# Attention stage of a two-layer gated cross-attention kernel: gate folded into the reciprocals, result addition on GpSimd, row statistics and maxima pieces placed anew

## The reference

```python
Q = _split_heads(query, H) * depth ** (-0.5)      # query = _layernorm(x), 2048 rows
K, V = halves of ctx_2048, 1601 rows, split into heads
logits = jnp.einsum('bhqd,bhkd->bhqk', Q, K) + b[0]
logits = logits + -1e+30 * (1.0 - mask)
weights = jax.nn.softmax(logits, axis=-1)
out = jnp.einsum('bhqk,bhkd->bhqd', weights, V)
...
x = x + jnp.tanh(g_xattn[1]) * _L1_xattn_ref(ctx_2048, _layernorm(x, axis=-1), mask_BxS2_ik0, L1_xattn_b)
```

## Time and profile before

| what | before |
|---|---|
| median of three executions | 1227.48 us (1226.67 to 1228.3) |
| the profiled execution, its own time | 1230.68 us |
| its span, first to last instruction | 1228.9 us |
| busy over the span: PE, DVE, ACT, POOL | 1099.3, 785.7, 532.3, 498.0 us |
| mean granted PE clock | 0.947 |
| the attention's first and last score matmul start | 411.0 and 852.0 us |

### The profile page before, as it was taken

The page is one execution under the profiler, slowest core; times in us unless marked ns, Lnnn a source line. Parts: engine busy times, 40 slices in busy tenths (PEclk is TensorE's granted clock), DMA queues, the critical chain, the costliest instruction groups (busy, mean ns, idle before and its releaser), DMA issues.

```text
span 1228.9 us, 20691 instructions
## 1 busy us (share of the span) xinstructions
PE 1099.3 (89%) x7126; PEld 826.5 (67%) x7126; DVE 785.7 (64%) x1804; ACT 532.3 (43%) x1145; POOL 498.0 (41%) x499
## 2 busy tenths in 40 slices
PE   4866999999967799999999999999983999999994
PEld 3665999999964444545455454544753999999994
DVE  5735767666659876767667676854339656565663
ACT  4141444433321345555565655565443333333341
POOL 1641111111104365857566676666002233434342
PEclk9966999999997889999999999999995999999998
DMA  6454787788832000000000000001623566666662
GB/s 225 94 148 182 317 318 289 302 322 336 339 131 86 1 1 1 1 18 1 1 1 18 2 1 2 18 22 50 220 73 112 162 181 211 183 208 198 192 210 57
DMA packets 52754, 160.71 MB, mean 131 GB/s; under 512 B 7434, under 2 KB 38540, under 8 KB 41644
## 3 DMA queue, kind: packets, MB, share of 16 engines
q1 hardware_dynamic: 38590, 138.42, 31.1%
q0 software_dynamic: 12000, 18.36, 6.4%
q10 hardware_dynamic: 2062, 2.60, 0.6%
HBM read 142.97 MB, written 16.38 MB: 130 GB/s over the span
## 4 chain that ended last, share of the span: by engine, by line
PE 78%; DVE 10%; issue 3%; ACT 2%; DMA 1%; POOL 1%; DVEq 0%; ACTq 0%; POOLq 0%
PE PQ L456 25%; PE PB L602 8%; PE PQ L587 7%; PE PB L483 6%; PE PB L569 5%; PE PB L592 4%; DVE Z L1046 4%; PE PB L332 4%; PE PB L502 3%; PE PQ L569 3%; PE PB L482 3%; PE PB L501 2%; PE PQ L643 1%; PE PQ L645 1%; PE PQ L644 1%
## 5 line engine op out<-in xcount | busy, mean ns | idle before, releaser
L1046 DVE TENSOR_REDUCE Z<-PB 128x1 f32<-128x402 f32 x319 | 172.3, 568 | 73.2 <-PE PB L569 71.6
L587 PE MATMUL PQ<-QS,KS 128*128 128x512 f32 x416 | 173.8, 433 | 3.3 <-ACT Z L1315 2.0
L456 PE MATMUL PQ<-Z,WS 128*128 128x128 f32 x1472 | 174.6, 278 | 0.5 <-ACT Z L1227 0.5
L456 PEld LDWEIGHTS PQ<-Z,WS 128*128 128x128 f32 x1472 | 173.1, 194 | 2.2 <-ACT Z L1227 0.9
L1242 ACT ACTIVATE Z<-PQ,W 128x128 f32<-128x128 f32 x312 | 89.0, 368 | 160.0 <-PE PQ L456 160.0
L456 PEld LDWEIGHTS PQ<-Z,W 128*128 128x128 f32 x1248 | 153.4, 194 | 4.8 <-ACT Z L1227 0.9
L456 PE MATMUL PQ<-Z,W 128*128 128x128 f32 x1248 | 154.3, 277 | 1.0 <-issue 0.5
L587 PEld LDWEIGHTS PQ<-QS,KS 128*128 128x128 f32 x416 | 77.1, 189 | 103.2 <-issue 67.7
L1315 ACT ACTIVATE Z<-PQ 128x512 f32<-128x512 f32 x208 | 109.8, 603 | 82.9 <-PE PQ L587 82.8
L1315 ACT ACTIVATE WS<-PQ 128x512 f32<-128x512 f32 x208 | 109.7, 604 | 82.6 <-PE PQ L587 82.4
L569 PE MATMUL PB<-KS,QS 128*128 128x402 f32 x319 | 119.1, 383 | 16.0 <-DVE Z L1046 7.0
(11 more groups left out here) (307 smaller groups left out, 2080.2 us busy)
## 6 DMA issues: line engine op xcount, KB each, us to landing
WS<-in_w SPq DMA_DIRECT2D x23, 2048.0 KB, 7.8
W<-in_w SPq DMA_DIRECT2D x39, 1028.0 KB, 5.1
WS<-in_w SPq DMA_DIRECT2D x23, 1024.0 KB
W2G<-in_w SPq DMA_DIRECT2D x8, 1024.0 KB, 9.3
xn<-WS SPq DMA_DIRECT2D x32, 128.0 KB, 1.8
X<-in_x SPq DMA_DIRECT2D x4, 512.0 KB, 12.1
WS<-yd SPq DMA_DIRECT2D x4, 512.0 KB, 5.1
out<-X SPq DMA_DIRECT2D x4, 512.0 KB, 2.8
```

Source lines behind the costliest of these rows:

```text
L456: t = e.matmul(bank[:, j * P:j * P + P], w[:, k, o:o + P], FXT[i % 2][:, k * P:k * P + P], start=k == 0, stop=k == 1)
L587: e.matmul(PB[g % 3], KS[:, 4 * (n % 2) + hh, kc * P:kc * P + P], QS[n % 2][:, hh, :], start=True, stop=True).then_inc(t_s, 1)
L1046: e.tensor_reduce(MP[j % 2][:, i:i + 1], PB[bank_of["pc", r]][:, 0:PIECE], AX.X, ALU.max).then_inc(v_pc, 1)
```

## The change

- The gate tanh(g) (`tg[:, 1:2]`) is multiplied into the 128x16 reciprocals by a new DVE tensor_scalar behind the reciprocal; `v_rt` is now signalled by it.
- Part 2 leaves DVE. GpSimd adds the scaled result to x (a tensor_tensor of 128x512) at the same place (3, 1), that is between its second and third addition of step 3. The semaphore is now `p_x3`.
- The four statistics move from (4, 0) to (4, 3) to (5, 1), (7, 1), (9, 1) and (11, 1).
- The pieces of the steps 0 to 11 were 5, 5, 6, 5, 5, 6, 5, 5, 6, 5, 5, 6 and are 7, 5, 4, 6, 4, 6, 5, 6, 5, 6, 5, 5. Both sum to 64.

```diff
-            parts = {(2, 0): 0, (2, 1): 1, (3, 1): 2, (4, 0): 4, (4, 1): 5, (4, 2): 6, (4, 3): 7}
+            parts = {(2, 0): 0, (2, 1): 1, (3, 1): 2, (5, 1): 4, (7, 1): 5, (9, 1): 6, (11, 1): 7}
+            pieces = (7, 5, 4, 6, 4, 6, 5, 6, 5, 6, 5, 5)
...
-                left = (5, 5, 6)[kc % 3] if kc < NK - 1 else 0
+                left = pieces[kc] if kc < NK - 1 else 0
...
             def into_x(n, part):
                 qg, hf = divmod(n, 2)
-                v = X[:, 4 * qg:4 * qg + 4, hf * P:hf * P + P]
                 if part == 0:
                     e.wait_ge(t_rec, n + 1)
-                    e.reciprocal(RT, PB[7].rearrange("p (g d) -> p g d", d=32)[:, :, 0]).then_inc(v_rt, 1)
+                    vc.step(e, e.reciprocal(RT, PB[7].rearrange("p (g d) -> p g d", d=32)[:, :, 0]))
+                    e.tensor_scalar(RT, RT, tg[:, 1:2], None, ALU.mult).then_inc(v_rt, 1)
...
-                elif part == 2:
-                    e.wait_ge(v_ot, n + 1)
-                    e.scalar_tensor_tensor(v, OT.rearrange("p (c d) -> p c d", c=4), tg[:, 1:2], v, ALU.mult,
-                                           ALU.add).then_inc(v_x3, 1)
                 elif part >= 4 and hf:
-                    e.wait_ge(v_x3, n + 1)
+                    e.wait_ge(p_x3, n + 1)
                     stats(4 * qg + part - 4)
...
+            def into_x(n, part):
+                if part == 2:
+                    qg, hf = divmod(n, 2)
+                    v = X[:, 4 * qg:4 * qg + 4, hf * P:hf * P + P]
+                    e.wait_ge(v_ot, n + 1)
+                    e.tensor_tensor(v, v, OT.rearrange("p (c d) -> p c d", c=4), ALU.add).then_inc(p_x3, 1)
+
+            interleaved(maxima, scores, lambda *a: None, lambda n: None, lambda n: None, into_x, lambda c: None)
+            into_x(7, 2)
```

More of the change, by code:

```diff
@@ L247, in build @@
             sem(n) for n in ("v_x2", "v_qn", "p_q", "t_q", "a_q", "t_pc", "v_pc", "v_m", "t_m", "a_m"))
-        t_s, a_p, p_acc, t_v, a_ot, a_rec, t_rec, v_rt, t_ot, v_ot, v_x3 = (
-            sem(n) for n in ("t_s", "a_p", "p_acc", "t_v", "a_ot", "a_rec", "t_rec", "v_rt", "t_ot", "v_ot", "v_x3"))
+        t_s, a_p, p_acc, t_v, a_ot, a_rec, t_rec, v_rt, t_ot, v_ot, p_x3 = (
+            sem(n) for n in ("t_s", "a_p", "p_acc", "t_v", "a_ot", "a_rec", "t_rec", "v_rt", "t_ot", "v_ot", "p_x3"))
         t_xr, v_xr, v_xg, v_rw, t_hr, a_hr, t_lm, v_lt, t_lt = (
@@ L1319, in attended @@
                 if n:
-                    e.wait_ge(v_x3, n)
+                    e.wait_ge(p_x3, n)
                 e.activation(OT, PB[6], ACT.Copy).then_inc(a_ot, 1)
@@ L1471, in scores @@
                     e.tensor_tensor(acc, acc, PT[g % 16], ALU.add).then_inc(p_acc, 1)
-            interleaved(maxima, scores, lambda *a: None, lambda n: None, lambda n: None, lambda n, part: None, lambda c: None)
+            def into_x(n, part):
[6 more added lines that the diff above has]
+            into_x(7, 2)
             power(rst[:, 12:NC], 11)
@@ L1587, in finished @@
             def finished(g):
-                e.wait_ge(v_x3, 2 * g + 2)
+                e.wait_ge(p_x3, 2 * g + 2)
                 e.dma_start(out[P + 512 * g:P + 512 * g + 512, :].rearrange("(c p) d -> p c d", p=P),
```

## The result

| | kernel before | changed kernel |
|---|---|---|
| median of 5 runs each, same chip | 1226.67 us (1225.93 to 1228.3) | 1245.8 us (1244.26 to 1251.75) |
| ratio, with 95% interval | | 1.0165 [1.0143, 1.0186] |
| profiled execution: own time, span | 1230.7, 1228.9 | 1251.75, 1249.6 |
| first to last score matmul of the stage | 852.01 - 410.97 = 441.04 | 873.46 - 409.32 = 464.14 |

The kernel is slower by 19.1 us; forecast were 10.6 more, 1238.1. The direction was right, and the measured median lies above the upper end of the range, 1242.0. The profiled execution of the changed kernel is 5.95 above its median (two of its five executions took 1251.7, three 1244.3 to 1245.8).

What follows compares the result with a forecast made beforehand. PE's issue was taken to bound the kernel, matmuls waiting for banks. Three passes at +1.13 and three with statistics at +2.39 sum to +10.6, so the median 1227.5 becomes 1238.1 us; range 1230.0 to 1242.0.

Steps and rivals of the forecast that it cites:

- PE's third piece starts at 3.61: +1.09.: Step 2: the gate's tensor_scalar waits for POOL's fourth addition, so PE's third piece starts 1.09 us later.
- Pass 7 has no pieces: nothing: Pass 7, the last of the attention stage: the change costs nothing there.
- GpSimd's addition to x: ... Nothing.: POOL's step 3: 1.25 us of added work delays later additions and the query tile, at no cost; 1.25 a pass if POOL were full.
- Step 0, +1.59: Step 0, 5 to 7 pieces: pieces and query transposition wait for reductions, so the values start 1.59 us later.
- Step 4, -0.36: Step 4, 5 to 4 pieces: the fifth piece saves 0.36 us, about a record of an unhindered piece.
- Step 1, -0.65: Step 1, 5 pieces with the transposition gone: saves 0.65 us, bounds -0.3 and -1.0; the step becomes 4.40.
- Steps 3, 7, 8 with 9, and 11 with 12: Changed piece counts: step 3 +0.48, step 7 +0.44, step 8 -0.48, step 9 +0.48, step 11 -0.48, step 12 -0.16 us.
- The two rules of the sixth piece: A sixth piece costs 0.48 us in short and long steps; DVE work behind a six-piece step's second reduction delays it.
- Statistics, net +1.26: Passes 2, 4 and 6: step 4 loses 0.70, steps 5 and 9 +0.55 each, step 7 +0.22, step 11's split +0.64 us.
- Nothing (bounds -0.4 and +0.5): Pass 0, held by DVE's other work until step 5: no change in time.
- The product does not wait: Rival, step 2: the tensor_scalar slips in ahead of POOL's fourth addition or is not held; +5.1, 1232.6 us; chance 0.20.
- The added pieces hide: Rival: added pieces in steps 0, 3, 7 and 9 cost less and statistics are hidden; -4.8, 1222.7 us; chance 0.12.

Runs made afterwards that it cites:

- the filled kernel: Changed kernel with nine repeats of the third score matmul of step 2 in passes 1 to 6, filling PE's wait; 1241.82 us, ratio 1.0109.
- the one with the statistics in step 12: Kernel before with reciprocal and multiplication ahead of step 2's first piece, and all four statistics in step 12; 1217.24 us, ratio 0.9917.
- old pieces: Changed kernel with the piece counts of the kernel before; 1244.66 us, ratio 1.0135.
- gate product alone: Kernel before with the gate's tensor_scalar behind the reciprocal and a plain addition to x left on DVE; 1241.22 us, ratio 1.0113.
- DVE's addition: Changed kernel with the plain addition to x back on DVE at (3, 1), GpSimd's taken out; 1250.77 us, ratio 1.0184.
- no product: Changed kernel without the gate's tensor_scalar; row sums taken with 1/tanh(g) in place of the ones; 1236.34 us, ratio 1.0074.
- pieces alone: Kernel before with the new piece counts alone; 1237.67 us, ratio 1.0068.
- statistics alone: Kernel before with the statistics moved to steps 5, 7, 9 and 11 alone; 1228.47 us, ratio 0.9999.

## Why the prediction was off

By its own steps, as measured in pass 3 and, for the terms of the statistics, pass 2:

- *"PE's third piece starts at 3.61: +1.09."* **This is the step that failed.** The product's length, 0.93, and its end with POOL's fourth addition are nearly as forecast (1 us or more), the third piece starts at 3.53, and PE stood still for 2.24 ("waits over 2 us"). But the wait was priced at full clock. PE then ran for 3.4 us at 1.2 GHz, once a pass, which costs 8.5 us in six passes by the trace of the filled kernel, and 5.0 by the medians. In the trace before, the waits at this place were 1.2 us, and the clock beside them was full; the forecast doubled the wait and kept the clock. No term of the sum and no bound of the range had a slow clock in it. The trace before had the sign, in pass 0, step 3: PE waits 2.30 there, and the clock is 0.50 right behind it. Its timeline of PE, and the clock of 430.5 to 433.8 in a busy line by stretch:

```profile
429.78 1.05 PE L569 MATMUL PB<-KS,QS 128*128 128x402 f32 x2 [2.30 <-DVE Z L1046]
430.76 1.94 PE L602 MATMUL PB<-WS,V 128*32 128x512 f32 x8
...
430.50:433.80 3.30, 3.30 (x17) 0.60 (x16) 2.26 (x6) 0.00 (x0) 3.15 (x6) 0.50 0.00 0
```

- *"Pass 7 has no pieces: nothing"* and *"GpSimd's addition to x: ... Nothing."* In the passes 1 to 6 the latter held. In pass 7 the addition fills POOL's gap in which DVE splits the router's weights, and this costs +3.4, a slow stretch included.
- *Step 0, +1.59:* +1.72 in pass 3, +1.86 in pass 2. *Step 4, -0.36:* -0.17; the fifth piece of that step is worth PE's own time, the lower bound, and not the record of an unhindered piece. *Step 1, -0.65:* -0.57. Together some 2.9 us in six passes, all of it upward.
- *Steps 3, 7, 8 with 9, and 11 with 12:* within 0.02 at full clock (step 3 by the filled kernel). The two rules of the sixth piece, and that work behind a reduction is free only in steps of five pieces, carried over.
- *Statistics, net +1.26:* passes 2 and 4 are 2.17 and 2.14 above pass 3 in the changed kernel, and were 0.72 above it before. That is +1.45 and +1.42; the term was 0.2 short, though its own steps hold (step 9 at 5.08, step 7 at 5.56, step 12 at 3.70): pass 2 is longer by 0.14 in step 0 and by 0.10 in steps 2 and 3, which have no statistic.
- *Pass 0, "Nothing (bounds -0.4 and +0.5)":* 61.32 against 63.65. It says little of the change: the kernel with the statistics moved alone, which in pass 0 runs the same instructions as the kernel before, had 59.84, and the one with the statistics in step 12 had 61.92. Pass 0 varies by up to 4 us from trace to trace, so the bounds of 0.4 and 0.5 were too narrow.
- *"The product does not wait", 0.20:* no. It took 0.93 us in the passes 1 to 6 of the changed kernel, and 1.03 with the old pieces, against 0.24 with POOL idle. *"The added pieces hide", 0.12:* no, 0.43 to 0.48 in the steps 3, 7 and 9, and 1.72 and more for the two of step 0.
- *The sum:* without a slow stretch in the passes 1 to 6 (the filled kernel) it is 14.15 by the medians and not 10.6. Of the smaller misses pass 7 (+3.4) and the steps 0, 1 and 4 (+2.9) went one way, and pass 0 and the rest of the program (-2.3 and -2.4, in these two traces) the other. That these largely cancel is luck.

**The rule of the skill** cited ahead (the Trainium skill, SBUF — State Buffer, "Who interferes with whom": whoever issues first holds the shared pair of ports for the whole instruction) agrees with what was seen: in all six kernels that have the product it ended, in the passes 1 to 7, within 0.04 us of an addition on POOL that had started before it, and the pair in pass 7, a cast and a subtraction with two SBUF inputs, went from 0.68 and 1.23 to 1.63 and 2.19 when POOL's rest was gone. No run shows a product that starts ahead of POOL's addition. What was missing in the forecast is a look at *every* DVE instruction that a moved POOL instruction can now meet, in all the passes.

What stays open: why some waits of over 2 us brought the slow clock and others did not (gate product alone, pass 1; DVE's addition, passes 2 and 4; old pieces, passes 1 and 5; no product, pass 7). And the traces and the medians agree only to some us (20.7 against 19.1 in all; 8.5 against 5.0 for the filled kernel). One trace a kernel is thin ground for a total: what lies behind the stage took from 372.2 to 380.5 us in the thirteen traces, and pass 0 from 59.8 to 63.7.

## What to carry to other kernels

Where PE has little slack, price a longer wait twice: the time it stands still, and the matmuls behind it at half the clock; here 1 us more of waiting cost 2.5 a pass by the traces (14.8 us in six). Ahead of putting even the smallest tensor_scalar into a chain that PE waits for, look at what POOL has begun by then, and when an instruction moves onto POOL, look at what DVE did in the gaps it closes, also in the first and last passes. A chain that frees a bank belongs ahead of the work that only uses the bank, and work without a deadline in a step that has no such chain: these two moves were worth 0.8%.

## What the runs showed of the hardware that was not expected

- One wait of PE of 2.2 to 2.4 us in step 2, in a stage in which it is busy 96% of the time in the kernel before (470 to 830 us), was followed by 3.4 us at 1.2 GHz in 19 of 24 passes (the four kernels with the product and this wait: 6, 5, 4 and 4 of 6); waits of 1.2 us at the same place never were (kernel before, pieces alone, statistics alone and no product, passes 1 to 6). Filled by matmuls whose results are thrown away, the same stretch kept the clock at 1.00.
- A 128x16 tensor_scalar on DVE, 0.24 us with POOL idle, took 0.93 to 1.18 beside additions of POOL.
- A cast of 128x1024 on DVE took 0.68, 0.98 or 1.63 us, and the subtraction behind it 1.23 or 2.19, as POOL's additions lay beside them.
